# Where the value bias is added, and where logits, GpSimd's and SyncE's first steps stand, in a fused attention and expert kernel

## The reference

```
q = layernorm(x) @ Wq + bq;  k = ctx @ Wk + bk;  v = ctx @ Wv + bv
x = x + softmax(mask(q k^T / 16)) v
t = layernorm(x)
scores = sigmoid(l2norm(t) @ l2norm(gate_w)^T)          # 16 experts
combine = top 8 of scores, divided by their sum, 0 elsewhere
routed = sum_e combine_e * (silu(t @ w_gate_e) * (t @ w_up_e)) @ w_down_e
shared = silu(t @ sw_gate) * (t @ sw_up) @ sw_down
out = x + routed + shared
```

## Time and profile before

| | |
|---|---|
| time, median of 3 runs | 662.44 us (659.66 to 663.13) |
| the profiled execution's own time | 664.48 us |
| its span | 662.4 us |
| granted TensorE clock, mean | 0.992 |
| TensorE busy | 637.2 us, 96% |
| TensorE's weight loads | 554.1 us, 84% |
| VectorE busy | 487.1 us, 74% |
| ScalarE busy | 236.2 us, 36% |
| GpSimd busy | 294.5 us, 44% |
| share of TensorE in the chain that ended last | 78% |

### The profile page before, as it was taken

One profiled execution on the slowest core, in us unless ns is written; L12 is line 12 of the kernel. 1 busy time (PEld: TensorE's weight loads), 2 busy tenths in 40 slices (PEclk: granted clock), 3 DMA queues, 4 the chain that ended last, 5 costly groups with the idle time before them and its releaser, 6 DMA issues.

```text
span 662.4 us, 10466 instructions
## 1 busy us (share of the span) xinstructions
PE 637.2 (96%) x3688; PEld 554.1 (84%) x3688; DVE 487.1 (74%) x941; ACT 236.2 (36%) x500; POOL 294.5 (44%) x275
## 2 busy tenths in 40 slices
PE   7897799999999999999999999999999999999997
PEld 7576688888888898888888898888888889888886
DVE  3777589876878688785888778686787768675444
ACT  5644334333233332424233332423333342333221
POOL 2517368623563336533544336533355334424443
PEclk9998979999999999999999999999999999999999
DMA  7264635143242442253240533343331630224100
GB/s 207 67 178 166 174 105 135 19 192 103 69 92 85 129 145 67 33 193 95 72 97 19 176 103 94 67 132 104 126 70 28 193 103 33 64 83 143 63 1 32
DMA packets 112654, 67.17 MB, mean 101 GB/s; under 512 B 80996, under 2 KB 102396, under 8 KB 112604
## 3 DMA queue, kind: packets, MB, share of 16 engines
q1 hardware_dynamic: 111516, 65.74, 34.8%
q10 hardware_dynamic: 1088, 0.79, 0.4%
HBM read 55.79 MB, written 10.42 MB: 100 GB/s over the span
## 4 chain that ended last, share of the span: by engine, by line
PE 78%; DVE 11%; ACT 4%; issue 3%; POOL 2%; DMA 2%; SPq 1%; POOLq 0%; ACTq 0%; DVEq 0%
PE gate_ps L384 8%; PE gate_ps L383 8%; PE up_ps L384 8%; PE up_ps L383 8%; PE gate_ps L382 8%; PE up_ps L382 8%; PE y_ps L382 8%; PE y_ps L383 7%; PE y_ps L384 7%; DVE hs L1144 3%; PE f_ps L527 2%; DVE route L1109 1%; DVE hidden L1138 1%; ACT hs L862 1%; DVE hidden L1134 1%
## 5 line engine op out<-in xcount | busy, mean ns | idle before, releaser
L1340 POOL TENSOR_TENSOR hidden<-hidden,cb 128x512 f32<-128x512 f32 x128 | 191.0, 1494 | 261.8 <-DVE hidden L1138 230.2
L855 ACT ACTIVATE hidden<-gate_ps 128x512 f32<-128x512 f32 x136 | 81.1, 597 | 290.8 <-PE gate_ps L384 290.8
L1134 DVE SCALAR_TENSOR_TENSOR hidden<-hidden,gate_ps 128x512 f32<-128x512 f32 x136 | 92.5, 680 | 98.1 <-ACT hidden L855 97.9
L382 PE MATMUL y_ps<-W,hs 128*128 128x256 f32 x544 | 154.3, 284 | 7.3 <-DVE hs L1144 7.3
L383 PE MATMUL y_ps<-W,hs 128*128 128x256 f32 x544 | 152.5, 280 | 0.0
L384 PE MATMUL y_ps<-W,hs 128*128 128x256 f32 x544 | 152.2, 280 | 0.0
L1144 DVE TENSOR_TENSOR hs<-hidden,hs 128x512 fp32r<-128x512 f32 x136 | 117.1, 861 | 25.6 <-ACT hs L862 25.4
L382 PEld LDWEIGHTS y_ps<-W,hs 128*128 128x128 f32 x544 | 103.2, 190 | 14.6 <-issue 6.6
L382 PE MATMUL gate_ps<-xT,W 128*128 128x512 f32 x272 | 108.7, 400 | 0.0
L383 PEld LDWEIGHTS y_ps<-W,hs 128*128 128x128 f32 x544 | 103.7, 191 | 5.0
L384 PE MATMUL gate_ps<-xT,W 128*128 128x512 f32 x272 | 107.3, 394 | 0.0
(11 more groups left out here) (162 smaller groups left out, 677.1 us busy)
## 6 DMA issues: line engine op xcount, KB each, us to landing
cb<-c_rows SPq DMA_DIRECT2D x64, 512.0 KB, 4.8
blocks<-in_x_dram SPq DMA_DIRECT2D x28, 128.0 KB, 3.0
xin<-in_x_dram SPq DMA_DIRECT2D x7, 512.0 KB, 4.0
t_rows<-blocks SPq DMA_DIRECT2D x28, 128.0 KB, 2.7
xs<-t_rows SPq DMA_DIRECT2D x7, 512.0 KB, 3.5
out_dram<-x SPq DMA_DIRECT2D x7, 512.0 KB, 7.0
p_rows<-blocks SPq DMA_DIRECT2D x28, 80.0 KB, 2.3
stage<-in_L_ffn_w_gate_dram SPq DMA_DIRECT2D x16, 128.0 KB, 2.3
```

Source lines behind the costliest of these rows:

```text
L382: mm(ps, lh, rh, start=first and i == 0, stop=False)
L855: af(ew[:, i, :], gate_ps[:, i, :], ACT.Tanh, scale=0.5).then_inc(tanh_done, 1)
L1134: V_.scalar_tensor_tensor(out=ew[:, i, :], in0=ew[:, i, :], scalar=1.0, in1=gate_ps[:, i, :], op0=ALU.add, op1=ALU.mult).then_inc(silu_don ...
L1340: pg.tensor_tensor(h[:, i, :], ew[:, i, :], cb[:, pair % PLACES, (e - 1) % 2, :], ALU.mult) \
```

## The change

The bias is added to the values where they lie after their product, once a batch, by VectorE (`bias_values`): for batch 0 together with all tails (128 x 512), for the others 128 x 256. ScalarE's copies of the high halves wait for it (v_biased). `add_bv` and its wait go. The tails' halves are made in two parts: batch 0's own ahead of the probabilities, `vt` behind them, and `move_v_tails` waits for the second. SyncE stores the probabilities of chunk 1 behind load 10, and loads them back behind load 11; the broadcasts of pairs 4 and 5 and the loads 7 to 11 stand in another order. GpSimd's `ln1_std(1, ...)` stands behind `weighted(0, 1)`. Logits and the router's steps are half a step earlier (top_eight and weights a whole one), ln1 of chunk c + 2 two steps.

```diff
-PE_AT = dict(scores=(0, .5), attend=(5.5, 6), logits=(12.5,), turn_z=(13,), turn_c=(15,))
-ACT_AT = dict(exps=(1.5, 2), probs_hi=(5,), t2_hi=(11.5,), read_z=(13,), tanh_scores=(13.5,), combine_rows=(15.5,))
+PE_AT = dict(scores=(0, .5), attend=(5.5, 6), logits=(12,), turn_z=(12.5,), turn_c=(14.5,))
+ACT_AT = dict(exps=(1.5, 2), probs_hi=(5,), t2_hi=(11.5,), read_z=(12.5,), tanh_scores=(13,), combine_rows=(15,))
 DVE_AT = dict(maxes=(.5, 1.5), swap_p=(2.5,), sum_reciprocal=(3.5,), probs_lo=(5,), residual=(6, 6.5),
-              ln2=(6.5, 7), ln2_scale=(8, 8.5), swap_x2=(8.5,), t2_lo=(11.5,), sum_logits=(13.5,), top_eight=(14.5,),
-              weights=(14.5,))
+              ln2=(6.5, 7), ln2_scale=(8, 8.5), swap_x2=(8.5,), t2_lo=(11.5,), sum_logits=(13,), top_eight=(13.5,),
+              weights=(13.5,))
-DVE_SOON = dict(ln1=(12, 12.5), swap_x=(15.5,))
-POOL_SOON = dict(add_bias=(9.5,), ln1_std=(13.5, 13.5), add_bv=(14.5, 15.5))
+DVE_SOON = dict(ln1=(10, 10.5), swap_x=(15.5,))
+POOL_SOON = dict(add_bias=(9.5,), ln1_std=(11.5, 11.5))
+POOL_FIRST = dict(ln1_std=(.5, .5))
...
@@ SyncE
-                sp.wait_ge(vt_split, 4)
+                sp.wait_ge(vt_split, 2)
...
-            for e in range(EARLY + 2, NE):
+            load_stage(EARLY + 2)
+            load_stage(EARLY + 3)
+            spread(0, PLACES)
+            load_stage(EARLY + 4)
+            load_stage(EARLY + 5)
+            store_probs(1)
+            load_stage(EARLY + 6)
+            load_probs(1)
+            spread(0, PLACES + 1)
+            for e in range(EARLY + 7, NE):
                 load_stage(e)
-                if e % 2 == 0 and PLACES + (e - EARLY - 2) // 2 < PAIRS:
-                    spread(0, PLACES + (e - EARLY - 2) // 2)
-                if e == EARLY + 6:
-                    move_probs(1)
+                if e % 2 == 1:
+                    spread(0, PLACES + 2 + (e - EARLY - 8) // 2)
...
@@ ScalarE
             def write_v_hi(b, ps):
-                act.wait_ge(v_made, b + 1)
+                act.wait_ge(v_biased, b + 1)
...
+            def vt_hi_first():
+                act.wait_ge(v_biased, 1)
                 for row in (0, PAD):
                     ins = af(Vtail[row:row + PAD, 0, :], y_ps[0:PAD, 0, D:2 * D], ACT.Copy)
-                ins.then_inc(vt_split, 1)
+                ins.then_inc(vt0_split, 1)
+
+            def write_vt_hi():
+                act.wait_ge(v_lo, 1)
                 af(vt[:, HI, :], y_ps[:, 0, D:2 * D], ACT.Copy).then_inc(vt_split, 1)
...
             exps(0, 0)
-            write_vt_hi()
+            exps(0, 1)
+            vt_hi_first()
             write_v_hi(0, y_ps[:, 0, 0:D])
-            exps(0, 1)
             probs_hi_first(0)
             probs_hi_first(1)
+            write_vt_hi()
...
-            write_v_hi(1, y_ps[:, 0, 0:D])
             bias_row_rest()
             router_hi()
+            write_v_hi(1, y_ps[:, 0, 0:D])
             split_hi(3)
...
@@ VectorE
+            def bias_values(b, ps):
+
+                dve.wait_ge(v_made, b + 1)
+                if b == 0:
+                    dve.wait_ge(bv_loaded, 16)
+                    dve.wait_ge(vt_made, 1)
+                V_.tensor_tensor(ps, ps, bvb[:].unsqueeze(1).broadcast_to([P, ps.shape[1], D]), ALU.add) \
+                    .then_inc(v_biased, 1)
...
-                dve.wait_ge(x_biased, upto(c, 2, q + 1))
...
             mask_and_max(0, 1)
+            bias_values(0, y_ps[:, 0, :].rearrange("p (t d) -> p t d", d=D))
             router_scaled()
-            write_vt_lo()
+            vt_lo_first()
             write_v_lo(0, y_ps[:, 0, 0:D])
             sum_reciprocal(0)
             probs_lo_first(0)
             probs_lo_first(1)
+            write_vt_lo()
...
             ln2_scale(0, 1)
+            bias_values(1, y_ps[:, 0:1, 0:D])
...
             silu_up(0, 1)
+            bias_values(2, f_ps[:, 0:1, 0:D])
             hidden_lo(0, 0)
...
             split_lo(4)
+            bias_values(3, f_ps[:, 1:2, 0:D])
             ln1(1, 0)
...
@@ GpSimd
-            add_bv(0, 0)
-            add_bv(0, 1)
...
             weighted(0, 0)
-            ln1_std(1, 0)
-            ln1_std(1, 1)
-            add_bv(1, 0)
-            add_bv(1, 1)
...
                     if ahead:
                         front(s + .5, c + 1)
+                    if c == 0:
+                        first(s + .5)
```

More of the change, by code:

```diff
@@ L168, in xattn_moe_kernel @@
                              "kt_read", "a_made", "a_read", "bq_spread", "brow_made", "brow_scaled", "v_made",
[L169 removed]
+                             "v_biased", "v_hi", "v_lo", "vt_made", "vt0_split", "vt_split", "vt_loaded", "gate_summed", "gate_inv", "gate_scaled", "gate_turned",
                              "gate_split", "keep_set", "pads_set", "bias_first", "w_hi", "w_lo_dve", "w_lo_pool"))
[L172 removed]
+        (ln1_stats, ln1_rstd, x_swapped, p_swapped, x2_swapped, t1_turned, t1_read, bias_added, scored, scaled, maxes, maxed, exped,
          rsummed, p_turned, p_hi, p_lo, attended, x2_made, ln2_stats, ln2_rstd, inv_norms, ln2_done, t2_turned, t2_hi,
@@ L175, in xattn_moe_kernel @@
          c_read, bn_step, pool_step, std_step, norm_step) = (
-            sem(n) for n in ("ln1_stats", "ln1_rstd", "x_swapped", "p_swapped", "x2_swapped", "t1_turned", "t1_read", "bias_added", "x_biased", "scored",
+            sem(n) for n in ("ln1_stats", "ln1_rstd", "x_swapped", "p_swapped", "x2_swapped", "t1_turned", "t1_read", "bias_added", "scored",
                              "scaled", "maxes", "maxed", "exped", "rsummed", "p_turned", "p_hi", "p_lo", "attended",
@@ L252, in load_x_blocks, with store_probs @@
                     sp.dma_start(x_blocks[p * SQ:(p + 1) * SQ], rows[c, p]).then_inc(x_blocked, 16)
-            def move_probs(c):
+            def store_probs(c):
                 sp.wait_ge(p_swapped, c)
@@ L261, in move_probs, with load_probs @@
                         .then_inc(p_stored, 16)
+            def load_probs(c):
                 sp.wait_ge(p_stored, upto(c - 1, 64, 64))
@@ L343, in _ @@
             spread(0, 3)
-            for e in range(EARLY + 2, NE):
-                load_stage(e)
-                if e % 2 == 0 and PLACES + (e - EARLY - 2) // 2 < PAIRS:
-                    spread(0, PLACES + (e - EARLY - 2) // 2)
-                if e == EARLY + 6:
-                    move_probs(1)
-            for pair in range(PLACES + (NE - EARLY - 2) // 2, PAIRS):
-                spread(0, pair)
+            load_stage(EARLY + 2)
[8 more added lines that the diff above has]
+            for e in range(EARLY + 7, NE):
+                load_stage(e)
+                if e % 2 == 1:
+                    spread(0, PLACES + 2 + (e - EARLY - 8) // 2)
+            assert PLACES + 2 + (NE - EARLY - 8) // 2 == PAIRS
             for c in range(CHUNKS):
@@ L356, in _ @@
                     if ahead:
-                        move_probs(c + 1)
+                        store_probs(c + 1)
+                        load_probs(c + 1)
                     for pair in range(PLACES + 1, PAIRS):
@@ L478, in values @@
                     pe.wait_ge(v_lo, 1)
-                    pe.wait_ge(vt_split, 4)
+                    pe.wait_ge(vt_split, 2)
                 elif b == 2:
@@ L1295, in add_bias @@
                                  .broadcast_to([P, TILES, KEYS]), ALU.add).then_inc(bias_added, 1)
-            def add_bv(c, q):
-                if c == 0:
-                    pool.wait_ge(bv_loaded, 16)
-                    pool.wait_ge(t1_turned, q + 1)
-                pool.wait_ge(ln1_stats, upto(c, 2, q + 1))
-                xh = xin[:, 2 * q:2 * q + 2, :]
-                pg.tensor_tensor(xh, xh, bvb[:].unsqueeze(1).broadcast_to([P, 2, D]), ALU.add).then_inc(x_biased, 1)
             def ln1_std(c, q):
@@ L1348, in front, with first @@
                     inverse_norm(c)
+            def first(at):
+                for part in due(POOL_FIRST, "ln1_std", at):
+                    ln1_std(1, part)
             def soon(at, c):
@@ L1355, in soon @@
                     ln1_std(c, part)
-                for part in due(POOL_SOON, "add_bv", at):
-                    add_bv(c, part)
             pool.sem_inc(h_done, FREE)
```

13 lines of the change are left out of this document (6 added, 7 removed).

## The result

| | before | after |
|---|---|---|
| median of the runs, us | 662.32 (659.65 to 665.04, 7 runs) | 655.12 (653.85 to 656.19, 7 runs) |
| profiled execution, own time / span, us | 664.48 / 662.4 | 653.85 / 651.4 |
| busy TensorE / VectorE / GpSimd, us | 637.2 / 487.1 / 294.5 | 632.0 / 467.2 / 275.0 |

The ratio is 0.9898, with a 95% interval of 0.9871 to 0.9924: the change makes the kernel faster by about 1%. The forecast was 651 with a range of 646 to 659.5.

A forecast was written before the change was run, and what follows sets the result against it. TensorE was taken to bound the steady periods (busy 75.7 of 76.4 us), with chunk 0 losing time to waits. From the profiled 664.5, minus 7.2 and 4.0 gave 653.3; less 2.04 for the median, forecast 651, range 646 to 659.5.

The forecast's parts named there:

- The start: Opening of chunk 0: later tail transfers, a clock fall and bias_values together cost 4.9 us.
- The tails' term: SyncE's tail transfers start 2.7 us later, delaying weight 3 and the first logits as much; ends 1.8 and 3.3.
- The term for bias_values: The bias additions on VectorE in chunk 0 cost 0.2 us in all; ends 0 and 1.9.
- The clock's fall: TensorE's 3.2 us idle at the first logits lowers its clock; price 1.5 to 3.3 us or nothing, taken 2.0.
- GpSimd's first steps: Chunk 0: without add_bv ahead of weighted(0, 1), down(0, 1) has no wait or slow clock; later waits from 60.46 go too.
- The probabilities and SyncE's order: Chunk 1's attention: swap ready about 65.9, store issued sooner, TensorE's wait 0.7 us, start at 78.3; gain 4.5 us.
- From the attention to chunk 2's scores: Stretch forecast at 53.4 us, including 1.0 for late logits; chunk 2's scores at 131.7, 7.2 us earlier than before.
- The steady periods: Earlier logits and router steps remove the routing-weights wait, 0.67 us in each of 6 periods: -4.0; ends 0 and -4.2.
- (a): Chunk 1's attention: probabilities still late, TensorE waits 2 us or more and the clock falls; 656 us, chance 0.18.
- (b): Start of the kernel costs nothing much, as the tails' delay hides or the clock stays up; 647 us, chance 0.12.
- (c): Chunk 0 stays as long as before because VectorE paces it; 659 to 660 us, chance 0.10.
- (d): Router's block ahead of silu_up(16) makes down(15) wait 2.5 us for VectorE each period; 672 us, chance 0.05.

The follow-up runs named there:

- e1: Changed kernel with the nine V tail transfers issued behind the loads of expert weights 3 and 4; 651.36 us, ratio 0.9825.
- e7: Changed kernel with e1's edit, plus weight 3's split behind the logits copies and the second bias_values ahead of ln2_scale(0, 1); 649.87 us, ratio 0.9811.
- e2: Changed kernel with the step tables of the kernel before put back (logits, router steps, ln1); 655.81 us, ratio 0.9891.
- e5: Kernel before with only the changed kernel's order on SyncE's queue; 657.58 us, ratio 0.9931.
- e4: Kernel before with only GpSimd's first steps moved: ln1_std(1) behind weighted(0, 1), add_bv(1) at step 4; 659.70 us, ratio 0.9951.
- e3: Changed kernel with SyncE's queue order of the kernel before from load 7 on; 661.69 us, ratio 0.9977.
- e6: Kernel before with only the changed kernel's step tables, add_bv kept at steps 14.5 and 15.5; 658.11 us, ratio 0.9929.

## Why the prediction came out as it did, point by point

**Own time and median.** The sum was made against the profiled execution's 664.48 and gave 653.3. The profiled execution after took 653.85, so the sum is met within 0.6 us. That it is so close is partly luck: the start came out 1.5 us cheaper than its term, chunk 0 from there 0.8 dearer (-11.34 for -12.1) and the periods 1.0 dearer, and these errors cancel. But the median is 655.12, 4.1 above the 651 forecast. The profile of before was 2.2 above its median, and I carried that on; the profile of after is the fastest of its seven. The next point shows why.

**The start: +4.9, measured +3.38 in the profile.** The tails' term was the mis-sized one: forecast +2.7 with ends of 1.8 and 3.3, measured 3.39 at the logits. SyncE began 2.94 later, and ScalarE began on weight 3 2.35 us after the issuing of its last piece ended, not 1.90, so in all 3.39 later. The term for bias_values, "taken 0.2 in all", costs nothing at the logits here: ScalarE's wait for it ended first. It is a hidden cost all the same: with the tails out of the way it holds the logits by 0.92 (e1), and e7 wins that back. The clock's fall, taken 2.0, did not come in the profiled execution. It does come in others. The windows of e2's profile (columns of the earlier trace rows) stand behind the same wait at the logits:
```profile
38.00:39.00 1.00, 1.00 (x4) 0.62 (x3) 0.24 (x1) 0.00 (x0) 0.00 (x0) 0.50 0.00 0
```
The same window after, and there all from 33 to 43 us:
```profile
38.00:39.00 1.00, 1.00 (x6) 0.82 (x5) 0.05 (x1) 0.56 (x3) 0.00 (x0) 1.00 0.00 0
```
In e2 it was low from 37.9 to 41.3, 3.4 us, and the scores start 1.52 later than after (51.60 against 50.08; 0.2 of it was there from the opening, so about 1.3 for the clock, where I had 2.0). Of the seven executions after, two have a mean granted clock of 0.999 or 1.0 and take 653.85 and 654.34; five have 0.996 or 0.997 and take 654.91 to 656.19. In e1 all four have 0.999 or more, and in e7 all six have 1.0. That the five lost their clock at this place is inferred: the means fit (half of 3.4 us in 654 is 0.0026), but only profiled executions show where. So the term was right in kind and a third too large, and it belongs to the median and not to the profile.

**GpSimd's first steps.** "With it goes its slow clock. The next waits at 60.46 and after it [...] go as well": the first half held (57.59, no wait), the second failed. The waits at `down(0, 2)` (1.40) and in front of 66.02 (1.03) stay: VectorE's own queue makes them (after, it is busy without a gap from 51.65 to 60.48, the end of the hidden_lo that `down(0, 2)` needs), and, as e5 shows, they hardly depend on how fast `down(0, 1)` runs. With the start 3.4 us late, what GpSimd's order brings is used up here: `down(0, 2)` at 60.63. Alone, in e4, it is worth 3.4 us.

**The probabilities and SyncE's order.** The attention was forecast at 78.3 with a wait of 0.7 and came at 78.64 without one. VectorE's last piece of the probabilities stands ahead of it:
```profile
77.34 0.68 DVE L1097 TENSOR_TENSOR ptail<-xn,ptail 32x512 fp32r<-32x512 f32 x1
```
It ends at 78.02, 0.6 us early, so TensorE's own work since `down(0, 3)` at 66.02 sets the start. The path to it was partly wrong. I expected the swap ready at 65.9; it was ready at 67.17, no earlier than before, since it hangs on the waits of the paragraph above. The lost 1.3 was made good by the store: 2.64, the low end of my bounds, where I had reckoned with something between. With the start as late as it now is, all of the gain at the attention is SyncE's order: e3 loses it (83.39, of which 1.5 is its later start), and e5 has it from that order alone.

**From the attention to chunk 2's scores: 53.4, measured 52.16.** I had allowed 1.0 for late logits, and no such wait shows. Scores of chunk 2 at 130.80, forecast 131.7 (131.5 when counted from the starts in the timeline, 0.16 ahead of the windows' edges).

**The steady periods: -4.0, measured -3.0.** Size nearly right, cause wrong. The step that failed is "it sat behind a GpSimd operation; with add_bv away and `weighted` done at 198.4 it should take 0.2". It does take 0.2 after, but because it moved; with add_bv away alone it takes 1.29 (e2), and the wait is gone all the same. The operation that mattered was hidden_lo(14), 1.46 beside add_bv. The missing microsecond is one period, 130.80 to 207.60. VectorE after, then GpSimd:
```profile
169.06 2.79 DVE L1029 TENSOR_SCALAR xn<-x,meanvar,small 128x256 f32<-128x256 f32 x2
```
```profile
168.88 1.42 POOL L1361 TENSOR_TENSOR hidden<-hidden,cb 128x512 f32<-128x512 f32 x1
170.26 1.44 POOL L1323 TENSOR_TENSOR keepb<-keep,brow 128x616 f32<-128x616 f32 x1
```
The second half of ln2_scale takes 2.79 us: it starts 0.18 after `weighted`, and the add_bias on its heels holds it too. One period later the pair starts 0.34 ahead of `weighted`, and takes 1.78, as in the later periods and in the kernel before:
```profile
245.49 1.78 DVE L1029 TENSOR_SCALAR xn<-x,meanvar,small 128x256 f32<-128x256 f32 x2
```
```profile
245.83 1.29 POOL L1361 TENSOR_TENSOR hidden<-hidden,cb 128x512 f32<-128x512 f32 x1
247.09 1.45 POOL L1323 TENSOR_TENSOR keepb<-keep,brow 128x616 f32<-128x616 f32 x1
```
The wait of 0.98 at 175.98 follows in VectorE's queue. e2 has the same 2.79 and a period of 76.88; e6, with add_bv, has 1.78 and 75.79. One step further back, VectorE's product at 167.19 waits 0.48 us for TensorE's `up`, in the kernel before 0.12 at the same place of the period, and that puts ln2_scale 0.37 later in the period. This long second period, 76.8 to 76.9, is in all five kernels without add_bv (after, e1, e2, e3, e7) and in none of the four with it (76.4 in before, e4 and e5, 75.8 in e6), whatever the steps and SyncE's order. So it goes with the moved bias or with the start that came with it; why `up` is answered later there stays open.

**The rivals.** (a), late probabilities, didn't happen with SyncE's new order; it is what e3 shows without it. (b), a start without cost, is half true of the clock and untrue of the tails: the start cost 3.4 us, and e7 shows that it need not. (c), chunk 0 as long as before, fell (11.3 us shorter), though VectorE does pace `down(0, 2)`. (d), `down(15)` waiting for the router's block, showed in no period.

**What each part is worth.** SyncE's order 5.3 alone (e5) and 5.8 to 6.6 as the last one added (e3). GpSimd's order 3.4 alone (e4). The steps 4.8 alone (e6), of which 3.3 in the steady periods, and nothing on top of the rest (e2). The V tails' place minus 3.8 to 4.6 (e1). The moved bias was not run by itself. These don't add up to 7.2, and need not: GpSimd's and SyncE's orders both bring the attention forward, each by about 4 us alone, the first by a TensorE that comes earlier (3.21 of the 4.20 us of waiting stay), the second by taking the wait away (0.43 stays); and the steps and the removal of add_bv cure one and the same steady wait.

## What to carry to other kernels

Where a value now arrives later, ask what stands behind its consumer in the queue that moves it: nine small transfers, 2.9 us later, held up two weight loads that had nothing to do with them, and gave back more than a third of what the rest of the change won (3.8 of 11.0). And look for the wait that stands just behind the longest one: bias_values cost nothing until the tails were moved. When an operation is slow beside another engine, look up the neighbour's line in the same window before naming the culprit, and follow the lost time through every queue in which it waits; the score operation (1.30, once 0.2) drew the eye, and hidden_lo(14), two engines upstream of the wait, was the one that mattered. A sum made against a profiled execution predicts another profiled execution; how far its median lies from that (2.2 below in the kernel before, 1.3 above after) is a term of its own.

## What the runs showed of the hardware

The same wait of TensorE had two outcomes. After 3.58 us at the logits the clock stayed at 1.00 in one profile and stood at 0.50 (1.2 GHz) for 3.4 us in e2's; after 2.03 us at `down(0, 1)` it stood at 0.50 in the profile of before and not in e5's. What a gap costs is therefore a chance, here 5 in 7 by the mean clocks (4 in 5 in e2), and nothing at all where another engine sets the next start.

The four stores of the probabilities had two prices of issuing: 2.6 to 2.7 us, or 4.2 to 4.7. It isn't load 11's place alone, since e6 has SyncE's order of before and took 2.70. SyncE's queue in e6:
```profile
67.66 0.42 SPq L292 DMA_DIRECT2D cb<-c_rows  x1
68.96 0.38 SPq L235 DMA_DIRECT2D stage<-in_L_ffn_w_gate_dram  x1
...
70.40 2.70 SPq L259 DMA_DIRECT2D p_rows<-blocks  x4
```
In e6 load 11 was issued 0.9 us after the transfer ahead of it; in e3, as in e4 and the kernel before, seven transfers were issued ahead of the stores without such a pause. One by one the four stores took 0.60, 0.64, 1.95 and 1.39 us in the kernel before, and 0.60 and three times 0.64 in the changed kernel: the price falls on the last two. That these stores slow down behind such a run fits all nine kernels, but no run varied it by itself, and it is no matter of the number alone: in the changed kernel the loads behind the four stores, the eighth to tenth transfer of a run, took 0.57, 0.49 and 0.47.

An execution can end late without any engine's doing: from the issue of the last output transfer to the end of the span passed 2.1 us in seven of the nine profiles, 3.9 in e3's and 4.4 in e5's.
